# Weight column groups taken in pairs: two 512-column groups per pass in the V, proj and FFN products, and two-tile instead of four-tile row groups in the FFN phase

## The reference

```python
x = x + _layernorm(_L0_attn_ref(_layernorm(x), qkv_w, proj_w, proj_b))
x = x + _layernorm(_L0_ffn_ref(_layernorm(x), weight, gamma, beta, ln_weight, ln_bias))
# attention: qkv = x @ qkv_w.T; masked softmax over a window; out @ proj_w.T + proj_b
# ffn: xn = layernorm(x) * ln_weight + ln_bias
#      out = einsum(xn, sign(weight)) * max(abs(weight)) * gamma + beta
```

## Time and profile before

| what | us |
|---|---|
| median of 3 runs | 1697.07 (1697.02 to 1728.95) |
| the profiled execution | 1693.06 |
| its span, slowest core (3) | 1691.5 |
| spans of the eight cores | 1680.9 to 1691.5 |
| TensorE matmul busy | 946.3 (56%) |
| VectorE busy | 596.5 (35%) |
| ScalarE busy | 302.4 (18%) |
| GpSimd busy | 320.9 (19%) |
| HBM read and written per core | 122.98 MB and 16.78 MB |

### The profile page before, as it was taken

The page is one execution under the profiler, slowest core; times in us unless marked ns, Lnnn a source line. Parts: engine busy times, 40 slices in busy tenths (PEclk is TensorE's granted clock), DMA queues, the critical chain, the costliest instruction groups (busy, mean ns, idle before and its releaser), DMA issues. The chain is left out here.

```text
span 1691.5 us, 12746 instructions; the slowest of 8 cores (1680.9 to 1691.5 us)
## 1 busy us (share of the span) xinstructions
PE 946.3 (56%) x4432; PEld 438.4 (26%) x4432; DVE 596.5 (35%) x822; ACT 302.4 (18%) x436; POOL 320.9 (19%) x207
## 2 busy tenths in 40 slices
PE   1267777777488837767766754888000233666300
PEld 1123333333233313333333321333000112222100
DVE  3611111111111233333333321222636876223586
ACT  2410000000000013223223230000414141222012
POOL 0000000000000044654654640000000404000532
PEclk9998999999799965555555555999555566777755
DMA  3232222231622000000000006240666100223052
GB/s 103 100 125 100 100 100 101 101 116 57 199 100 100 0 28 1 0 1 1 1 0 1 1 1 223 100 150 0 212 260 226 72 1 0 100 100 132 17 198 99
DMA packets 37872, 140.57 MB, mean 83 GB/s; under 512 B 2082, under 2 KB 2082, under 8 KB 27170
## 3 DMA queue, kind: packets, MB, share of 16 engines
q1 hardware_dynamic: 34498, 117.61, 19.9%
q0 software_dynamic: 3312, 22.15, 3.4%
HBM read 122.98 MB, written 16.78 MB: 83 GB/s over the span
## 5 line engine op out<-in xcount | busy, mean ns | idle before, releaser
L379 PE MATMUL qk<-lnT,wbf 128*128 128x512 bf16 x1280 | 258.8, 361 | 80.0 <-DVE wbf L40 80.0
L379 PEld LDWEIGHTS qk<-lnT,wbf 128*128 128x128 bf16 x1280 | 111.5, 102 | 227.3 <-issue 126.6
L441 PE MATMUL vp<-vwbf,lnT 128*128 128x512 bf16 x576 | 132.6, 395 | 38.2 <-DVE vwbf L40 38.2
L858 PE MATMUL ep<-fwbf,xnT 128*128 128x512 bf16 x512 | 117.5, 393 | 50.0 <-ACT fwbf L829 49.4
L713 PE MATMUL dp<-pwbf,lnT 128*128 128x512 bf16 x512 | 118.9, 397 | 40.3 <-DVE pwbf L40 40.3
L947 PE MATMUL tpe<-identb,lnbf 128*128 128x128 bf16 x128 | 15.3, 304 | 213.7 <-DVE lnbf L933 194.3
L479 POOL DMA_DIRECT2D maskm<-masks x1 | 0.7, 674 | 595.8 <-PE sp L503 595.8
L503 PE MATMUL sp<-KT,QT 64*128 64x144 bf16 x256 | 50.7, 274 | 107.9 <-DVE tstrip L518 101.8
L41 ACT COPY ptbuf<-tpc 128x512 bf16<-128x512 bf16 (+1 forms) x128 | 67.4, 578 | 180.7 <-PE tpc L596 180.7
L560 DVE TENSOR_REDUCE stats<-tstrip 128x16 f32<-128x2304 f32 x16 | 40.8, 2553 | 156.8 <-ACT tstrip L557 156.8
L566 POOL TENSOR_TENSOR pstrip<-tstrip,stats 128x2304 bf16<-128x2304 f32 x16 | 64.6, 4035 | 139.7 <-DVE tstrip L518 115.4
(11 more groups left out here) (94 smaller groups left out, 1044.4 us busy)
## 6 DMA issues: line engine op xcount, KB each, us to landing
wstage<-qk_strips SPq DMA_DIRECT2D x32, 1024.0 KB, 4.9
vstage<-v_w SPq DMA_DIRECT2D x8, 2048.0 KB, 10.9
pwstage<-proj_wt SPq DMA_DIRECT2D x8, 2048.0 KB, 10.9
fwstage<-ffn_wt SPq DMA_DIRECT2D x8, 2048.0 KB, 8.3
ybuf<-y_scratch SPq DMA_DIRECT2D x16, 1024.0 KB, 11.9
xbuf<-x_shard SPq DMA_DIRECT2D x8, 1024.0 KB, 6.4
xre<-x_shard SPq DMA_DIRECT2D x8, 1024.0 KB, 11.0
y_scratch<-x POOLq DMA_DIRECT2D x8, 1024.0 KB, 10.9
```

The source lines that it names most:

```text
L379: return lambda e: e.matmul(banks[gi][:, 0:wd], wbf[:, par * D + kc * 128: par * D + (kc + 1) * 128], lnT[:, kc * TOK + c0: kc * TOK + c0 ...
L441: return lambda e: e.matmul(vbanks[bpar][:], lnT[:, kc * TOK + 128 * vt: kc * TOK + 128 * vt + 128], vwbf[:, par * NGV + kc * 512: par * N ...
L858: return lambda e: e.matmul(ebanks[bpar][:], xnT[:, kc * 1024 + 128 * t: kc * 1024 + 128 * t + 128], fwbf[:, par * NGF + kc * 512: par * N ...
```

## The change

V, proj and FFN loop over two pairs of column groups (`np_`) rather than over four groups. Both groups of a pair are staged and cast before the pair's first matmul; both halves of the bf16 buffer hold one pair. For each k the stationary tile is used by two matmuls in a row, one for each group, into two of now four PSUM banks. In V and proj the staging buffer keeps its two slots of 2 MB. In the FFN `fwstage` gets two slots rather than one and `fwbf` is doubled; to make room, ybuf, scr_e and lnbf2 hold two tiles rather than four, and F1 and F3 loop over four pairs of tiles. F1 now multiplies groups 0 and 1 for its two tiles. F2 stages groups 2 and 3 and multiplies both. The statistics columns are renumbered. Bank copies alternate by `(t + j) % 2`. The number of matmuls, of transfers and of their bytes is the same.

```diff
-            for ng in range(4):
-                par = ng % 2
+            for np_ in range(2):
                 cast_last = 0
-                p.wait("v", "t", vwbf_rd_t[par])
-                for hh in range(2):
-                    slot = (ng * 2 + hh) % 2
...
+                p.wait("v", "t", vwbf_rd_t)
+                for j in range(2):
+                    ng = np_ * 2 + j
+                    for hh in range(2):
+                        slot = (ng * 2 + hh) % 2
+                        p.wait("q", "v", stage_rd_v[slot])
...
                 for vt in range(9):
...
                     for kc in range(16):
...
+                        for j in range(2):
+                            def mk(vt=vt, kc=kc, j=j, bb=b0 + j):
+                                return lambda e: e.matmul(
+                                    vbanks[bb][:],
+                                    lnT[:, kc * TOK + 128 * vt: kc * TOK + 128 * vt + 128],
+                                    vwbf[:, j * NGV + kc * 512: j * NGV + (kc + 1) * 512],
+                                    start=(kc == 0), stop=(kc == 15))
...
-        ybuf = eph.enter_context(nc.sbuf_tensor("ybuf", [128, 4 * D], F32))
-        scr_e = eph.enter_context(nc.sbuf_tensor("scr_e", [128, 4 * D], F32))
-        lnbf2 = eph.enter_context(nc.sbuf_tensor("lnbf2", [128, 4 * D], BF16))
+        ybuf = eph.enter_context(nc.sbuf_tensor("ybuf", [128, 2 * D], F32))
+        scr_e = eph.enter_context(nc.sbuf_tensor("scr_e", [128, 2 * D], F32))
+        lnbf2 = eph.enter_context(nc.sbuf_tensor("lnbf2", [128, 2 * D], BF16))
...
-        fwstage = eph.enter_context(nc.sbuf_tensor("fwstage", [128, 8 * 512], F32))
-        fwbf = eph.enter_context(nc.sbuf_tensor("fwbf", [128, 16 * 512], BF16))
+        fwstage = eph.enter_context(nc.sbuf_tensor("fwstage", [128, 2 * 8 * 512], F32))
+        fwbf = eph.enter_context(nc.sbuf_tensor("fwbf", [128, 2 * 16 * 512], BF16))
...
             emit_ffn_stage(0)
+            emit_ffn_stage(1)
...
-            for tq in range(0, NT, 4):
-                ts = list(range(tq, tq + 4))
+            for tpair in range(0, NT, 2):
+                ts = [tpair, tpair + 1]
...
-            for ng in range(1, 3):
-                emit_ffn_stage(ng)
-                emit_ffn_mms(ng, list(range(NT)))
+            emit_ffn_stage(2)
             emit_ffn_stage(3)
...
-                emit_ffn_mms(3, list(range(tq, tq + 4)))
-                ffn_done_q[tq] = (p.cnt["v"], p.cnt["s"])
+                emit_ffn_mms(1, [tpair, tpair + 1])
+                ffn_done_pair[tpair] = (p.cnt["v"], p.cnt["s"])
```

More of the change, by code:

```diff
@@ L435, in build_program @@
                 for vt in range(9):
-                    bpar = vt % 2
-                    eng_r, cnt_r = bank_rd[bpar]
-                    p.wait("t", eng_r, cnt_r)
+                    b0 = (vt % 2) * 2
+                    for bb in (b0, b0 + 1):
+                        eng_r, cnt_r = bank_rd[bb]
+                        p.wait("t", eng_r, cnt_r)
                     for kc in range(16):
[L440 to L446, removed]
@@ new lines, in build_program, with mkevac @@
+                    for j in range(2):
+                        ng = np_ * 2 + j
+                        eng = "v" if ((vt + j) % 2 == 0) else "s"
+                        p.wait(eng, "t", last_mm)
+                        if eng == "s":
+                            p.wait(eng, "g", c_zero)
+                        def mkevac(vt=vt, ng=ng, bb=b0 + j):
+                            return lambda e: _copy(e,
+                                VTOK[:, vt * D + ng * 512: vt * D + (ng + 1) * 512],
+                                vbanks[bb][:])
+                        c = p.emit(eng, mkevac())
+                        bank_rd[b0 + j] = (eng, c)
@@ L707, in build_program @@
                 for t in range(NT):
-                    bpar = t % 2
-                    eng_r, cnt_r = bank_rd[bpar]
-                    p.wait("t", eng_r, cnt_r)
+                    b0 = (t % 2) * 2
+                    for bb in (b0, b0 + 1):
+                        eng_r, cnt_r = bank_rd[bb]
+                        p.wait("t", eng_r, cnt_r)
                     for kc in range(16):
[L712 to L718, removed]
@@ new lines, in build_program, with mkev @@
+                    for j in range(2):
+                        ng = np_ * 2 + j
+                        p.wait("v", "t", mm_last)
+                        p.wait("v", projb_q)
+                        def mkev(t=t, ng=ng, bb=b0 + j):
+                            return lambda e: e.scalar_tensor_tensor(
+                                x1[:, t * D + ng * 512: t * D + (ng + 1) * 512],
+                                dbanks[bb][:], 1.0,
+                                projb[:, ng * 512:(ng + 1) * 512],
+                                ALU.mult, ALU.add,
+                                accum_out=accD[:, t * 4 + ng: t * 4 + ng + 1])
+                        c = p.emit("v", mkev())
+                        bank_rd[b0 + j] = ("v", c)
@@ L850, in emit_ffn_mms @@
                 for t in tlist:
-                    bpar = t % 2
-                    eng_r, cnt_r = ebank_rd[bpar]
-                    p.wait("t", eng_r, cnt_r)
+                    b0 = (t % 2) * 2
+                    for bb in (b0, b0 + 1):
+                        eng_r, cnt_r = ebank_rd[bb]
+                        p.wait("t", eng_r, cnt_r)
                     for (eng_x, c_x) in xnT_rdy[t]:
@@ new lines, in emit_ffn_mms, with mkev @@
+                    for j in range(2):
+                        ng = np_ * 2 + j
+                        eng = "v" if ((t + j) % 2 == 0) else "s"
+                        p.wait(eng, "t", mm_last)
+                        def mkev(t=t, ng=ng, bb=b0 + j):
+                            return lambda e: _copy(e,
+                                ffnstage[:, t * D + ng * 512: t * D + (ng + 1) * 512],
+                                ebanks[bb][:])
+                        c = p.emit(eng, mkev())
+                        ebank_rd[b0 + j] = (eng, c)
+                        ffn_rdy.setdefault(t, []).append((eng, c))
@@ L898, in build_program @@
                     p.wait("s", cqs[i])
-                    p.wait("s", "t", lnbf_rd_t[t % 4])
-                st1 = ln_stats2([(yas[i], ts[i] % 4, lbs[i]) for i in range(nts)])
+                    p.wait("s", "t", lnbf_rd_t[t % 2])
+                st1 = ln_stats2([(yas[i], ts[i] % 2, lbs[i]) for i in range(2)])
                 cv_ln2 = []
```

208 lines of the change are left out of this document (97 added, 111 removed).

## The result

The changed kernel takes 1728.5 us in the median of nine runs (forecast 1729). Over the kernel before, measured beside it, the ratio is 1.0173, with an interval of 1.0159 to 1.0187: slower, and by less than 2%. The medians count every run, while ratios and their intervals leave out runs in a slower state that any kernel of this kind falls into now and then (here one of the nine, at 1760.3 us). The profiled execution took 1727.54 us, its span was 1726.0 (1691.5 before), again on core 3.

A forecast was written before the change was run, and what follows sets the result against it. TensorE was taken to bound V and proj, chains and staging waits the FFN. V +12.4, proj +12.6, F1's start +3.7, F1 and F2 -18.1 and F3 +21.8 gave +32.4 on 1697.07: 1729 us, 8-in-10 range 1708 to 1749.

The forecast's parts named there:

- The matmul's price: All stages: 0.216 us per matmul stays, no gain from using a tile twice; bound 4 us on 1600 matmuls.
- V and proj: Both stages: exposed transfers and casts cost more than the removed gaps and starts save; +12.4 and +12.6 us.
- The gap term: V, between the pairs: the last two transfers start only after casts free their slots; a gap of 20.2 us.
- the first waits: V and proj, before the first matmul: four casts through two slots, +12.8 and +11.6 us.
- F1's start: Start of F1: 8 MB of weights rather than 4 ahead of two ybuf tiles; +3.7 us, between 0 and 8.3.
- F1 and F2: FFN: four F1 pairs of 48.0 us and one F2 gap of 22.6; 272.5 against 290.6, -18.1 us.
- the term for slow starts: TensorE: each start from idle costs extra, 2.1 us per start.
- F3: FFN's last stage: a pair's first product waits for the previous pair's store; cycle 33.9 us, +21.8 in all.
- the landing of the pair's first store: F3: with two loads and two stores under way, this store takes 9.2 us before the next pair's first product.
- The rival of cheaper exposures: F3, V, proj: pair's store lands in 6 us, staged transfers in 8.3; 1714 us; chance 0.07.
- The rival of the late store: F3: the pair's store is late, 3.2 us three times, +9.6, 1739 us; chance 0.32, alone or with longer transfers.
- The sum: Whole kernel: 12.4 + 12.6 + 3.7 - 18.1 + 21.8 = +32.4 us, a time of 1729; chance 0.46.

The follow-up runs named there:

- The kernel without reuse: The changed kernel with each group's 16 matmuls one after the other, so no stationary tile is used twice in a row: 1724.0 us, ratio 1.0152.
- the move of the product in F3: Combined kernel (casts moved, FFN paired, four parts in F3) with the next pair's product before a pair's last operations: 1640.9 us, against 1648.0 in plain order.

## Why the prediction was right, and where its terms were off

- **The matmul's price.** Right. The pitch and the one load per matmul stayed. The kernel without reuse shows no loss. The Trainium skill's 131 ns (page "TensorE: Matmul & The Clock Gate", section "Back-to-back issue gap") doesn't show here either: 64 matmuls at a granted clock of 1.00 take 13.97 us in F2, 0.218 each.
- **V and proj.** The mechanism was right. The measured costs alone, +9.9 and +12.9, stand beside +12.4 and +12.6. On core 3 of the profiled execution V cost 4.5 more than forecast: 1.3 in the first wait, 2.3 in the gap, 0.9 in the runs. The transfers were sized by the landings of the earlier trace rows, from one core of one execution. The gap term was good (20.0 in the median of the cores, forecast 20.2); the first waits were forecast 12.8 and 11.6 longer and came 13.8 and 14.0 longer in the median. Proj's had been sized by a landing of 9.3 us; the same transfer took 8.9 to 11.7 on the eight cores of the kernel before.
- **F1's start.** +3.7 forecast, +3.7 measured. It was the middle of a range of 8, so this is partly luck.
- **F1 and F2, mis-sized by 5.** The cycle of a pair was forecast as 48.0 and came as 48.4, 47.9 and 49.5; the one gap of F2 as 22.6 and came as 22.9. What was off is for the most part the term for slow starts: the four blocks of 64 matmuls in F1 took 14.59, 14.45, 16.07 and 15.20 us where I had 14.4, together 2.7 more, and F2's first block 16.59 where I had, with the start, 15.9. The rest is 0.3 in the gap and about 1.4 in drains and last copies in F2. The stretches of the timeline with their granted clock (the column behind the busy times; the first row is the transposes ahead of the third block):

```profile
1443.50:1448.30 4.80, 3.73 (x32) 3.23 (x33) 3.36 (x3) 1.04 (x2) 0.00 (x0) 0.50 0.01 3
1400.00:1415.00 15.00, 14.70 (x67) 6.32 (x64) 0.93 (x3) 1.66 (x3) 0.00 (x0) 0.95 0.00 0
1448.00:1464.00 16.00, 15.85 (x65) 6.68 (x64) 0.81 (x2) 1.60 (x2) 0.00 (x0) 0.86 0.00 1
1536.00:1553.00 17.00, 16.60 (x65) 6.81 (x66) 2.90 (x5) 0.90 (x2) 0.31 (x1) 0.84 0.34 123
1553.00:1567.00 14.00, 13.97 (x64) 6.14 (x64) 1.09 (x2) 0.86 (x2) 0.00 (x0) 1.00 0.00 1
```

  The same 64 matmuls at mean clocks of 0.95, 0.86, 0.84 and 1.00: after an idle stretch the engine is still at the lower of its two levels (0.50 of full speed) when the block begins, and for a time that varies, 14.5 to 16.6 us for the block. The number of such starts is not what changed: F1 has four instead of two, F2 one instead of three. What I overlooked is what stands in front of F1's blocks. Before, four tiles' transposes precede a block, the last 48 of their 64 matmuls within 7 us, and the two blocks took 14.67 and 13.97; now it is 32 within 5 us. Over the eight cores these blocks take 13.8 to 14.9 us before and 14.0 to 16.1 in the changed kernel. That the shorter run of transposes is the reason was not tried apart.
- **F3, mis-sized by 6 on core 3 and by 9 in the median, the other way.** The step that failed is the landing of the pair's first store, 9.2 us. On core 3 it is 6.3, 9.1 and 5.8; on the other seven cores all 21 such stores land in 5.6 to 6.4. The rest of the cycle was right to 0.5 us: sums at 13.4, store at 24.2. The rival of cheaper exposures had 6 for this store, and its price, 9.6 us less in F3, gives +12.2 where the median of the cores has +12.7: in F3 this rival came true, and core 3 hid it. Its other half did not come: the third and fourth 2 MB transfers took 9.7 to 12.1 us in V and 10.1 to 11.6 in proj, not 8.3. It had rested on fewer transfers in flight, which the rows fit (two loads and two stores now) but no run tests. The rival of the late store (12.4) did not come.
- **The sum.** On core 3 the stages' errors against the forecast are +4.5 in V, +1.8 in proj with the residual part, +5.0 in F1 and F2, -5.9 in F3, and -3.6 in stage B, which has no part in the change (and +0.2 in attention). They cancel to about +2: +34.5 on the spans where the forecast had +32.4. The time itself, 1729 against 1728.5, has a second cancellation: the profiled execution came 2.0 above the forecast's 1725.5, but the median is 1.0 above the profiled execution, not 4.0. So a sum that is right to 1 us was made of terms that are right to 6, or to 9 in F3, and that closeness is luck. The range of 20 us on either side was the honest part.

What stays open: whether the move of the product in F3 is worth the 3 us that it shows on seven of eight cores, and what sets the slow starts of F1's blocks. And it was not tried how V and proj would do with four staging slots.

## What to carry to other kernels

Pairing column groups to use a stationary tile twice pays only if the profile shows fewer weight loads or a lower pitch; here there was a load per matmul either way, and the price was 4 MB more in front of the first matmul of a stage, 13 to 14 us in V and again in proj. When a stage has gaps, look first at what stands behind what on the engine that ends them: casts whose data had long arrived stood behind the last bank copies, and moving the two of each group forward in the list gave 42 us, where pairing lost 28. When one execution of a kernel is read, look at all its cores: the slowest one, core 3 here, had landings that no other core had, and it hid which forecast of F3 was the right one. When a buffer is cut from four parts to two, look for the store whose landing now stands between one use and the next, and for a dead buffer that could serve as the missing parts.

## What was not expected of the hardware

- A GpSimd addition and a VectorE operation with two SBUF inputs took turns whole: 6.61 us for a 2.35 us operation beside an addition of 4.49. The Trainium skill says so ("SBUF — State Buffer", section "SBUF: two separate sides": the port pair they share is an exclusive lock for the whole instruction); the trace agrees. I had counted on it in F3's first pair, and for the moved product only as a rival.
- In F3 a store of 1 MB took 4.2 us when nothing else was under way, 5.6 to 9.3 in the changed kernel beside loads and one other store, and 5.7 to 13.8 in the first group of the kernel before beside loads and three others. The landing went with what was in flight, so a change in the grouping can change it; in the changed kernel the first store of a pair landed in about 6 us and the second in about 8.6.
- The time at the lower clock level after an idle stretch is not one number: the same block of 64 matmuls took 14.5, 16.1 and 16.6 us in the changed kernel, where it takes 13.97 at a granted clock of 1.00.
